# A graph attention layer on one Trainium2 core: the last score tile moves to ScalarE and GpSimd, mean and variance move to ScalarE, and half of the normalisation moves into the next step

## The chip, the cores and the metric

The kernel runs on one core of one Trainium2 chip. The metric is the device time of one execution in microseconds (us), the median over runs. The engines are named as in the profile: PE is TensorE, with PEld its weight loads, DVE is VectorE, ACT is ScalarE, POOL is GpSimd and SP is SyncE, which here only issues DMAs.

## The reference

For 16 graphs of N = 512 nodes with D = 384 features, 12 heads of E = 32, the layer computes (biases and constants left out where they play no part):

```python
h    = einsum('bnd,ade->bane', x, W)                      # features per head
th   = tanh(h)
attn = th @ w_src + swap(th @ w_dst)                      # one score per pair of nodes
attn = where(attn >= 0, attn, 0.2 * attn)                 # leaky
attn = softmax(where(adj, attn, -999))
out  = elu(einsum('banm,bame->bane', attn, h) + b)
gate = sigmoid(x @ H_w.T + H_b)
y    = x + gate * out + (1 - gate) * x
return (y - mean(y)) / sqrt(var(y) + 1e-5)                # over the 384 features
```

## The kernel before

One step handles one graph `b`, in C = 4 chunks of 128 nodes. There are 16 steps: `program` writes steps 0, 1, 14 and 15 out and loops over the others in pairs. Five engines each run their own fixed list of instructions; semaphores alone tie them together. Everything is software pipelined: in step `b` PE computes features of graph `b + 1` and gates of graph `b`, and what follows attention for graph `b - 1` (elu, gate mix, row sums, squares) is done in step `b`, with its normalisation in step `b + 1`.

**Score tiles.** For graph `b` the softmax numerators are 48 tiles of 128x512 (12 heads by 4 chunks), worked in 6 pairs of heads `j` (`edges`, L803). Tile t is one DVE instruction, `max(v, u) * adjacency` (L820), with the row `v` of a head spread over all partitions in `v_all` and the adjacency converted into PSUM by ACT. The tiles go through 16 slots (`ew`). PE multiplies each with the values (`attend`, L1068, L1082), ACT copies each pair's result (`copy_out`), PE transposes it, DVE divides (`attended`). Other DVE work is put between tiles by hand: `between` maps a place i of pair j to functions.

**From features to scores.** PE computes chunk 0 of the next graph's features at the head of a step, ACT takes the tanh (L471), POOL multiplies and halves (`weigh`, L296 and L302, four chunks), DVE reduces (`head_sums`, L782, at places between tiles), then the maximum over nodes (`scores_max`, L786). PE turns it (`max_T`, L1014) ahead of pair 2 of the attention.

**POOL's list in a step** (L386): four times `weigh`, the issue of a DMA that adds the bias, `subtract_x` and `mix` for graph `b - 1` (L339, L344, L347; the last of them writes `y` and waits for the store of the `y` before it), `add_rows` (L319, L323), `values`, `mean`, four times `split_low`, the issue of a second adding DMA, `variance`, `scale`. `add_rows` makes `hb_tot`, which PE reads in `means` (L1043, L1047). In PE's list `means` stands between the gates of chunk 3 and pairs 4 and 5 of the attention.

**SP's list** (L227): when `y` of graph `b - 1` is written, it loads `x_in`, stores the turned score rows to `v_rows`, waits until they have landed, and loads `v_all` for pairs 0, 1 and 2 of the next step (L220).

**ACT's list** (L580) holds tanh and copies of the features, two halves of `normalise` for graph `b - 2` around them, tanh and scaling of the gate, `copy_out`, copies of gates, `row_sums` and `row_squares` of graph `b - 1`, `split` and `adjacency`. The last step (`step_last` on each engine) has an order of its own and finishes graph 15 on DVE and POOL together.

Of the kernel before, what the change touches and what calls it, by code (L numbers as in the profile page):

```python
# [14 lines left out]
P = 128  # L15
# [6 lines left out]
def gat_layernorm(nc, x, xT, adjT, W, HwT, w_rows, bias, H_b, out):  # L22
# [23 lines left out]
    VB = 32  # L46
    assert N == 512 and H * E == D and B % 2 == 0

    ctx = ExitStack()
    with ctx:  # L50
# [6 lines left out]
        def sem(name):  # L57
# [7 lines left out]
        adj_in = sb("adj_in", [P, C, N], U8)  # L65

# [34 lines left out]
        u = sb("u", [P, 2, C, H])  # L101
        vals = sb("vals", [P, 2, C, H, VW])
# [49 lines left out]
            ew_ready ew_free outT_copied tr_done inv_done att_done  # L152
# [40 lines left out]
        def _(sp):  # L193
# [33 lines left out]
            def step(b, q, first, last, ahead=True):  # L227
# [11 lines left out]
                for j in range(VSLOTS, HP):  # L239
                    sp.wait_ge(S["ew_ready"], 4 * H * b + 2 * C * (j - 2))  # L240
                    load_v(b, q, j)
# [7 lines left out]
                if not last:  # L249
                    store_v(b + 1, 1 - q)  # L250
                    sp.wait_ge(S["st_v"], 64 * b + 128)
                    for j in range(VSLOTS):
                        if j:
                            sp.wait_ge(S["ew_ready"], 4 * H * b + 2 * C * (j + 4))
# [12 lines left out]
        def _(pool):  # L267
# [67 lines left out]

            def subtract_x(b):
# [24 lines left out]

# [4 lines left out]
            def step_last(b, q):  # L366
                subtract_x(b - 1)
# [15 lines left out]
                variance(b - 1)  # L383
                scale(b - 1)

            def step(b, q, first, last, ahead=True):  # L386
# [6 lines left out]
                if not last:  # L393
                    add_bias(b + 1)
                if first:
# [5 lines left out]
                if not last:  # L401
                    add_rows(b + 1, 1 - q)
                    values(b + 1, 1 - q)
                if not first:
                    mean(b - 1)
# [8 lines left out]
                if not first:  # L414
                    variance(b - 1)
                    scale(b - 1)
# [795 lines left out]
```

## Time and profile before

| what | value |
|---|---|
| median of 3 runs | 658.49 us (658.39 to 658.75) |
| the profiled execution, its own time | 658.69 us |
| its span, first to last instruction | 656.9 us |
| mean granted TensorE clock | 0.993 of 2.4 GHz |
| ACT busy | 429.6 us, 65% |
| chain that ended last | PE 48%, DVE 30%, issue 8%, POOL 7%, DMA 2%, ACT 2% |

The span is 1.79 us shorter than the profiled execution's own time. Busy time is the union of an engine's instructions; a matmul's end is modelled. Times of single instructions are counted from the start of the span, and L12 is line 12 of the kernel. "Rows" numbers in square brackets name the groups further down.

### The profile page before, as it was taken

The page shows a single profiled execution, that of the slowest core. Times are in us where ns is not written, and L with a number is a line of the kernel's source. Part 1 is how long each engine was busy: PE and PEld are TensorE (multiplying, and loading weights), DVE is VectorE, ACT ScalarE, POOL GpSimd, SP SyncE. Part 2 cuts the span into 40 slices and gives each one's busy share as a digit, 9 for nine tenths or more (in the row PEclk, how much of TensorE's full clock was granted, in tenths as well). Part 3 has the DMA queues.
Part 4 walks back from the last instruction along what each step waited for, and adds up shares of the span by engine and source line. Part 5 has one row for each costly group of instructions (what it writes and reads, how often), then busy time and mean ns, then how long its engine had stood idle before and what let it go on. Part 6 is the DMA issues. An engine that isn't in the chain of part 4 may idle for free.

```text
span 656.9 us, 12491 instructions
## 1 busy us (share of the span) xinstructions
PE 630.9 (96%) x3279; PEld 373.0 (57%) x3279; DVE 639.0 (97%) x1174; ACT 429.6 (65%) x936; POOL 571.4 (87%) x448
## 2 busy tenths in 40 slices
PE   8999999999999999999999999999999999999983
PEld 5565656574565647556664665656456565745531
DVE  7999999999999999999999999999999999999996
ACT  5434658486784848768485775848578584866664
POOL 2576998989989998998989999898999989997293
PEclk9999999999999999999999999999999999999997
DMA  6356549578475856848586584857747585675602
GB/s 209 118 131 181 178 123 274 128 196 248 140 235 129 235 164 176 240 146 251 133 210 190 154 238 144 249 132 200 228 142 233 139 259 126 187 211 131 217 40 97
DMA packets 54747, 117.62 MB, mean 179 GB/s; under 512 B 7106, under 2 KB 32452, under 8 KB 54724
## 3 DMA queue, kind: packets, MB, share of 16 engines
q1 hardware_dynamic: 42196, 81.56, 38.5%
q0 software_dynamic: 4320, 23.59, 19.2%
q10 hardware_dynamic: 8208, 12.19, 4.9%
q8 instruction: 11, 0.18, 0.1%
q14 instruction: 12, 0.10, 0.0%
HBM read 104.35 MB, written 12.98 MB: 179 GB/s over the span
## 4 chain that ended last, share of the span: by engine, by line
PE 48%; DVE 30%; issue 8%; POOL 7%; DMA 2%; ACT 2%; DVEq 1%; SPq 0%; POOLq 0%; ACTq 0%
PE out_T L1082 30%; DVE ew L820 20%; PE hg L982 13%; POOL th_w L296 4%; DVE sd L782 4%; DVE ex L842 3%; PE tr L1090 2%; POOL th_w L302 2%; PE hg L1047 1%; ACT th L471 1%; DMA xT_in<-in_xT 1%; DVE att L834 1%; DVEq L819 1%; PE hg L1014 1%; PE hg L1018 1%
## 5 line engine op out<-in xcount | busy, mean ns | idle before, releaser
L820 DVE SCALAR_TENSOR_TENSOR ew<-v_all,u,adj 128x512 f32<-128x512 f32 x768 | 522.7, 727 | 1.9 <-DMA v_all<-v_rows 1.2
L1082 PE MATMUL out_T<-ew,vals 128*64 128x512 f32 x1536 | 346.9, 597 | 0.0
L1082 PEld LDWEIGHTS out_T<-ew,vals 128*64 128x64 f32 x1536 | 106.3, 136 | 188.8 <-issue 144.1
L525 ACT ACTIVATE att_T<-out_T,out_bias 128x512 f32<-128x512 f32 x96 | 65.9, 686 | 116.1 <-PE out_T L1082 115.6
L296 POOL TENSOR_TENSOR th_w<-th,score_w 128x768 f32<-128x768 f32 x60 | 110.6, 1844 | 24.3 <-ACT th L471 24.3
L982 PE MATMUL hg<-w_hi,xT_hi 128*128 128x384 f32 x384 | 96.9, 360 | 0.8 <-ACT xT_hi L463 0.8
L982 PE MATMUL hg<-w_lo,xT_hi 128*128 128x384 f32 x384 | 88.2, 337 | 0.0
L982 PE MATMUL hg<-w_hi,xT_lo 128*128 128x384 f32 x384 | 87.7, 336 | 0.0
L302 POOL TENSOR_TENSOR th_w<-th_w 128x384 f32<-128x384 f32 x60 | 82.6, 1376 | 4.7
L982 PEld LDWEIGHTS hg<-w_hi,xT_hi 128*128 128x128 f32 x384 | 62.6, 189 | 40.2 <-issue 39.4
L982 PEld LDWEIGHTS hg<-w_lo,xT_hi 128*128 128x128 f32 x384 | 69.1, 188 | 0.0
L982 PEld LDWEIGHTS hg<-w_hi,xT_lo 128*128 128x128 f32 x384 | 68.9, 188 | 0.0
L333 POOL TENSOR_TENSOR vals<-h_sb,vals 128x384 f32<-128x384 f32 x64 | 53.3, 866 | 16.2 <-ACT vals L499 16.2
L339 POOL TENSOR_TENSOR ex<-ex,x_plus 128x1536 f32<-128x1536 f32 x15 | 56.4, 3758 | 11.4 <-ACT x_plus L530 11.4
L307 POOL TENSOR_TENSOR xT_lo<-xT_in,xT_hi 128x384 fp32r<-128x384 f32 x60 | 58.6, 1014 | 0.5 <-ACT xT_hi L463 0.5
L1090 PE MATMUL tr<-ident,att_T 128*128 128x128 f32 x384 | 53.1, 273 | 4.8 <-ACT att_T L525 4.8
L347 POOL TENSOR_TENSOR y<-x_in,ex 128x1536 f32<-128x1536 f32 x15 | 52.1, 3470 | 2.2 <-POOL ex L344 2.0
L344 POOL TENSOR_TENSOR ex<-gate,ex 128x1536 f32<-128x1536 f32 x15 | 52.0, 3467 | 1.4
L480 ACT ACTIVATE gate_tanh<-hg 128x384 f32<-128x384 f32 x60 | 29.5, 492 | 34.1 <-PE hg L982 32.8
L1090 PEld LDWEIGHTS tr<-ident,att_T 128*128 128x128 f32 x384 | 45.6, 141 | 10.8 <-ACT att_T L525 8.7
L471 ACT ACTIVATE th<-hg 128x384 f32<-128x384 f32 x64 | 31.7, 495 | 29.6 <-PE hg L982 29.6
L782 DVE TENSOR_REDUCE sd<-th_w 128x24 f32<-128x384 f32 (+1 forms) x64 | 36.5, 570 | 3.9 <-POOL th_w L302 3.7
(116 smaller groups left out, 669.0 us busy)
## 6 DMA issues: line engine op xcount, KB each, us to landing
v_all<-v_rows SPq DMA_DIRECT2D x95, 512.0 KB, 4.6
xT_in<-in_xT SPq DMA_DIRECT2D x16, 768.0 KB, 9.5
h_sb<-in_bias POOLq DMA_DIRECT2D x15, 768.0 KB, 6.7
x_in<-in_x SPq DMA_DIRECT2D x15, 768.0 KB, 4.6
gate_tanh<-in_H_b POOLq DMA_DIRECT2D x15, 768.0 KB, 9.4
out<-y ACTq DMA_DIRECT2D x15, 768.0 KB, 3.7
adj_in<-in_adjT SPq DMA_DIRECT2D x16, 256.0 KB, 9.8
v_rows<-v_turn SPq DMA_DIRECT2D x64, 6.0 KB
```

What stands on the lines that cost most here:

```text
L296: g.tensor_tensor(th_w[:, c % 2], th[:, c].unsqueeze(1).broadcast_to([P, 2, D]), score_w[:], ALU.mult).then_inc(S["thw_done"], 1)
L302: g.tensor_tensor(t[:, :, 0:E // 2], t[:, :, 0:E // 2], t[:, :, E // 2:E], ALU.add).then_inc(S["thh_done"], 1)
L307: g.tensor_tensor(xT_lo[:, q, :, n], xT_in[:, :, n], xT_hi[:, q, :, n].bitcast(F32), ALU.subtract).then_inc(S["xlo_done"], 1)
L333: g.tensor_tensor(o[:, :, 0:E], h_sb[:, c].rearrange("p (h e) -> p h e", e=E), o[:, :, E:E + 1].broadcast_to([P, H, E]), ALU.mult).then_in ...
L339: g.tensor_tensor(ex[:], ex[:], x_plus1[:], ALU.subtract).then_inc(S["mixed"], 1)
L347: g.tensor_tensor(y[:], x_in[:], ex[:], ALU.add).then_inc(S["mixed"], 1)
L525: a.activation(att_T[:, j % 2], OUT[j % 2][:], ACT.Identity, bias=out_bias[:, q, j:j + 1]).then_inc(S["outT_copied"], 1)
L782: ve.tensor_reduce(sd_ckh[:, 2 * H * c:2 * H * (c + 1)], t, AX.X, ALU.add).then_inc(S["sd_done"], 1)
L820: ve.scalar_tensor_tensor(out=twos(ew[:, (2 * C * j + i) % SLOTS, :]), in0=twos(v_all[:, j % VSLOTS, k]), scalar=u[:, q, c, h:h + 1], in1= ...
L982: last = te.matmul(o, l, r, start=(i == 0), stop=(i == len(mms) - 1))
L1082: te.matmul(OUT[j % 2][VW * k:VW * k + VW, :], vals[:, q, c, h, :], ew[:, t % SLOTS, :], start=(c == 0), stop=(c == C - 1)).then_inc(S["ew ...
L1090: last = te.transpose(TR[j % 2][:, c * P:(c + 1) * P], att_T[:, j % 2, c * P:(c + 1) * P], ident[:])
```

## The change

* **Tiles.** DVE makes 47 of the 48 tiles of a step (`EW` = 47). The last one (head 11, chunk 3) is made by ACT as Relu(v - u), then + u, after `copy_out` of pair 3, and POOL multiplies it with a bf16 copy of the adjacency, between `add_rows` and `values`. ACT makes that copy (`adjacency_side`) once a step. PE waits for POOL before that tile.
* **Mean and variance** become two ACT instructions (at the end of `row_sums` and of `row_squares`); POOL's three small ones go.
* **Next step.** Two of the four squares of `b - 1` move from the end of the step to where the second half of `normalise` stood in the next step. `scale` (power and shift) moves from the end of POOL's list to the next step, between the bias DMA and `subtract_x`; it runs in steps from 2 on. The whole `normalise` and the store of `y` move behind the copy of gate chunk 0.
* **Places on DVE.** In ordinary steps `head_sums` 0 goes one place later, `head_sums` 3 and `scores_max` one place earlier.
* **SP** counts 47 tiles, and the load for pair 2 also waits for ACT's part of the side tile.

```diff
+    SIDE = 1
+    EW = 4 * H - SIDE
...
+            def side_tiles(b):
+                pool.wait_ge(S["adj_side_done"], b + 1)
+                pool.wait_ge(S["side_scored"], 2 * SIDE * b + 2 * SIDE)
+                tiles = ew[:, SLOTS - SIDE:SLOTS, :]
+                g.tensor_tensor(tiles, tiles, adj_side[:].unsqueeze(1).broadcast_to([P, SIDE, N]), ALU.mult).then_inc(S["side_ready"], 1)
+
-            def mean(b):
-                pool.wait_ge(S["sums_done"], C * b + C)
-                g.tensor_tensor(neg_mean[:], sums[:], minus_share[:], ALU.mult).then_inc(S["mean_done"], 1)
-
-            def variance(b):
-                pool.wait_ge(S["squares_done"], C * b + C)
-                g.tensor_tensor(var[:], squares[:], share[:], ALU.mult).then_inc(S["var_done"], 1)
-                pool.wait_ge(S["var_done"], 2 * b + 1)
-                g.tensor_tensor(var[:], var[:], eps[:], ALU.add).then_inc(S["var_done"], 1)
-                pool.wait_ge(S["var_done"], 2 * b + 2)
-
             def scale(b):
-
+                pool.wait_ge(S["var_done"], b + 1)
+                if not isinstance(b, int) or b:
+                    pool.wait_ge(S["y_done"], C * b)
                 g.tensor_tensor(rstd[:], var[:], half[:], ALU.pow).then_inc(S["rstd_done"], 1)
                 pool.wait_ge(S["rstd_done"], 2 * b + 1)
                 g.tensor_tensor(shift[:], neg_mean[:], rstd[:], ALU.mult).then_inc(S["rstd_done"], 1)
 
             def step_last(b, q):
+                scale(b - 2)
...
+                if not isinstance(b, int) or b > 1:
+                    scale(b - 2)
...
                     add_rows(b + 1, 1 - q)
+                    side_tiles(b)
                     values(b + 1, 1 - q)
-                if not first:
-                    mean(b - 1)
...
-                if not first:
-                    variance(b - 1)
-                    scale(b - 1)
...
+            def side_tiles(b, q):
+                act.wait_ge(S["side_ready"], b)
+                a.activation(minus_u[:], u[:, q, C - 1, H - SIDE:H], ACT.Copy, scale=-1.0).then_inc(S["side_u"], 1)
+                act.wait_ge(ld_v[2], 32 * b + 32)
+                act.wait_ge(S["ew_free"], 4 * H * b + 4 * H)
+                act.wait_ge(S["side_u"], b + 1)
+                for i in range(SIDE):
+                    k = 2 - SIDE + i
+                    a.activation(ew[:, SLOTS - SIDE + i, :], v_all[:, 2, k], ACT.Relu, bias=minus_u[:, i:i + 1]).then_inc(S["side_scored"], 1)
+                for i in range(SIDE):
+                    h = H - SIDE + i
+                    act.wait_ge(S["side_scored"], 2 * SIDE * b + i + 1)
+                    a.activation(ew[:, SLOTS - SIDE + i, :], ew[:, SLOTS - SIDE + i, :], ACT.Identity,
+                                 bias=u[:, q, C - 1, h:h + 1]).then_inc(S["side_scored"], 1)
+
...
+                a.activation(neg_mean[:], sums[:], ACT.Copy, scale=-1.0 / D).then_inc(S["mean_done"], 1)
...
+                a.activation(var[:], squares[:], ACT.Identity, scale=1.0 / D, bias=eps[:, 0:1]).then_inc(S["var_done"], 1)
...
                 features(b + 1, 0)
-                if not isinstance(b, int) or b > 1:
-                    normalise(b - 2, 0, 2)
                 features(b + 1, 1)
                 elu_exp(b - 1, 1 - q)
                 features(b + 1, 2)
                 features(b + 1, 3)
                 if not isinstance(b, int) or b > 1:
-                    normalise(b - 2, 2, C)
+                    row_squares(b - 2, 2, C)
                 x_forms(b - 1)
                 gate_tanh_pass(b - 1)
                 copy_out(b, q, 0)
                 copy_out(b, q, 1)
                 gate_quarter_pass(b - 1)
                 gates(b, 0)
+                if not isinstance(b, int) or b > 1:
+                    normalise(b - 2)
                 gates(b, 1)
                 copy_out(b, q, 2)
                 exps(b + 1, 1 - q)
                 copy_out(b, q, 3)
+                side_tiles(b, q)
                 gates(b, 2)
                 row_sums(b - 1)
                 gates(b, 3)
...
-                row_squares(b - 1, 0, 2)
                 for c in range(2):
                     adjacency(b + 1, c)
+                adjacency_side(b + 1)
                 copy_out(b, q, 4)
-                row_squares(b - 1, 2, C)
+                row_squares(b - 1, 0, 2)
...
-                        put(5 if first else 1, lambda: head_sums(b + 1, 0))
+                        put(5 if first else 2, lambda: head_sums(b + 1, 0))
                         put(8 if first else 6, lambda: head_sums(b + 1, 1))
                     if j == 2 and not last:
                         put(3, lambda: head_sums(b + 1, 2))
-                        put(7, lambda: head_sums(b + 1, 3))
-                        put(8, lambda: scores_max(b + 1))
+                        put(7 if first else 6, lambda: head_sums(b + 1, 3))
+                        put(8 if first else 7, lambda: scores_max(b + 1))
...
-                        pe.wait_ge(S["ew_ready"], 4 * H * b + t + 1)
+                        if t < EW:
+                            pe.wait_ge(S["ew_ready"], EW * b + t + 1)
+                        elif t == EW:
+                            pe.wait_ge(S["side_ready"], b + 1)
```

## Rows read from the trace of the kernel before

**Rows 1.** The page: each engine's busy us, share of the span, instructions.

```profile
PE 630.9 (96%) x3279; PEld 373.0 (57%) x3279; DVE 639.0 (97%) x1174; ACT 429.6 (65%) x936; POOL 571.4 (87%) x448
```

**Rows 2.** Timeline of ACT: start, us, instruction, count, idle before and its end.

```profile
104.48 0.49 ACT L471 ACTIVATE th<-hg 128x384 f32<-128x384 f32 x1 [1.15 <-PE hg L982]
...
298.63 0.49 ACT L471 ACTIVATE th<-hg 128x384 f32<-128x384 f32 x1 [0.98 <-PE hg L982]
...
322.19 0.24 ACT L497 ACTIVATE s_pos<-d_rel 128x48 f32<-128x48 f32 x1
...
323.91 0.69 ACT L525 ACTIVATE att_T<-out_T,out_bias 128x512 f32<-128x512 f32 x1 [1.16 <-PE out_T L1082]
...
337.47 0.49 ACT L471 ACTIVATE th<-hg 128x384 f32<-128x384 f32 x1 [1.07 <-PE hg L982]
...
376.29 0.49 ACT L471 ACTIVATE th<-hg 128x384 f32<-128x384 f32 x1 [0.98 <-PE hg L982]
...
570.32 0.49 ACT L471 ACTIVATE th<-hg 128x384 f32<-128x384 f32 x1 [0.98 <-PE hg L982]
```

**Rows 3.** Waits of PE: us in total, times, longest.

```profile
PE hg L1014 <- DVE d_max_c L786: 8.3, 15, 0.7
```

**Rows 4.** Timeline of PE and of its weight loads.

```profile
82.95 0.33 PE L1014 MATMUL hg<-ident,d_max_c 128*128 128x128 f32 x1 [0.56 <-DVE d_max_c L786]
...
315.94 0.33 PE L1014 MATMUL hg<-ident,d_max_c 128*128 128x128 f32 x1 [0.49 <-DVE d_max_c L786]
...
327.64 0.81 PEld L1047 LDWEIGHTS hg<-mean_w,hb_tot 128*128 128x128 f32 x6
...
366.55 0.59 PEld L1047 LDWEIGHTS hg<-mean_w,hb_tot 128*128 128x128 f32 x4
```

**Rows 5.** Timeline of POOL, end of one step and the next.

```profile
296.73 1.03 POOL L362 TENSOR_TENSOR rstd<-var,half 128x4 f32<-128x4 f32 x1
297.84 0.20 POOL L364 TENSOR_TENSOR shift<-neg_mean,rstd 128x4 f32<-128x4 f32 x1
299.28 1.86 POOL L296 TENSOR_TENSOR th_w<-th,score_w 128x768 f32<-128x768 f32 x1 [1.24 <-ACT th L471]
...
304.12 2.55 POOL L302 TENSOR_TENSOR th_w<-th_w 128x384 f32<-128x384 f32 x1
...
313.04 3.78 POOL L339 TENSOR_TENSOR ex<-ex,x_plus 128x1536 f32<-128x1536 f32 x1
...
320.54 3.48 POOL L347 TENSOR_TENSOR y<-x_in,ex 128x1536 f32<-128x1536 f32 x1 [0.17 <-POOL ex L344]
...
325.90 1.02 POOL L323 TENSOR_TENSOR hb_tot<-hb_sum 128x384 f32<-128x384 f32 x1
```

**Rows 6.** Timeline of DVE.

```profile
302.27 0.55 DVE L782 TENSOR_REDUCE sd<-th_w 128x24 f32<-128x384 f32 x1 [0.30 <-POOL th_w L302]
...
304.05 1.75 DVE L842 SCALAR_TENSOR_TENSOR ex<-ex,att 128x1536 f32<-128x1536 f32 x1
...
328.57 9.37 DVE L820 SCALAR_TENSOR_TENSOR ew<-v_all,u,adj 128x512 f32<-128x512 f32 x14
...
333.90 0.75 DVE L820 SCALAR_TENSOR_TENSOR ew<-v_all,u,adj 128x512 f32<-128x512 f32 x1
```

**Rows 7.** DMA: SP's issues, then KB each and us from issue to landing.

```profile
329.55 4.70 SPq L220 DMA_DIRECT2D v_all<-v_rows  x3
...
v_all<-v_rows SPq DMA_DIRECT2D x1, 512.0 KB, 4.2
...
out<-y ACTq DMA_DIRECT2D x15, 768.0 KB, 3.7
```

**Rows 8.** Timeline of POOL and DVE near the end of the last step.

```profile
637.51 1.82 POOL L377 TENSOR_TENSOR ex<-ex,gate_tanh 128x768 f32<-128x768 f32 x1 [0.78 <-ACT ex L682]
...
641.37 1.82 POOL L382 TENSOR_TENSOR ex<-ex,x_plus 128x768 f32<-128x768 f32 x1
...
643.91 0.69 DVE L896 SCALAR_TENSOR_TENSOR ex<-ex,att 128x512 f32<-128x512 f32 x1 [0.21 <-ACT ex L686]
```

More of the change, by code:

```diff
@@ L65, in gat_layernorm @@
         adj_in = sb("adj_in", [P, C, N], U8)
+        adj_side = sb("adj_side", [P, N], BF16)
         w_hi = sb("w_hi", [P, KD, 2 * D], F32R)
@@ L101, in gat_layernorm @@
         u = sb("u", [P, 2, C, H])
+        minus_u = sb("minus_u", [P, SIDE])
         vals = sb("vals", [P, 2, C, H, VW])
@@ L239, in step @@
                 for j in range(VSLOTS, HP):
[L240 removed]
+                    sp.wait_ge(S["ew_ready"], EW * b + 2 * C * (j - 2))
                     load_v(b, q, j)
@@ L253, in step @@
                         if j:
-                            sp.wait_ge(S["ew_ready"], 4 * H * b + 2 * C * (j + 4))
+                            sp.wait_ge(S["ew_ready"], EW * b + min(2 * C * (j + 4), EW))
+                        if j == VSLOTS - 1:
+                            sp.wait_ge(S["side_scored"], 2 * SIDE * b + 2 * SIDE)
                         load_v(b + 1, 1 - q, j)
@@ L402, in step @@
                     add_rows(b + 1, 1 - q)
+                    side_tiles(b)
                     values(b + 1, 1 - q)
-                if not first:
-                    mean(b - 1)
                 if ahead:
@@ L413, in step @@
                 add_gate_bias(b)
-                if not first:
-                    variance(b - 1)
-                    scale(b - 1)
             def after():
@@ L442, in before @@
                     adjacency(0, c)
+                adjacency_side(0)
                 act.wait_ge(S["dve_setup"], DVE_SETUP)
@@ L503, in adjacency, with adjacency_side @@
                 if not isinstance(b, int) or b:
-                    act.wait_ge(S["ew_ready"], 4 * H * b - 2 * C + 4 * (c // 2) + 4)
+                    act.wait_ge(S["ew_ready"], EW * b + (0 if c // 2 else SIDE - C))
                 a.activation(ADJ_WORDS[c // 2][:, c % 2], adj_in[:, c].bitcast(U16), ACT.Copy).then_inc(S["adj_done"], 1)
+            def adjacency_side(b):
+                if not isinstance(b, int) or b:
+                    act.wait_ge(S["side_ready"], b)
+                a.activation(adj_side[:], adj_in[:, C - 1], ACT.Copy).then_inc(S["adj_side_done"], 1)
             def out_biases(b, q):
@@ L560, in row_sums @@
                     a.activation(scratch[:, c % 2], y[:, c], ACT.Copy, accum_out=sums[:, c:c + 1]).then_inc(S["sums_done"], 1)
+                act.wait_ge(S["sums_done"], C * b + C)
+                if not isinstance(b, int) or b:
+                    act.wait_ge(S["rstd_done"], 2 * b)
+                a.activation(neg_mean[:], sums[:], ACT.Copy, scale=-1.0 / D).then_inc(S["mean_done"], 1)
             def row_squares(b, lo=0, hi=C):
@@ L568, in row_squares @@
                                  accum_out=squares[:, c:c + 1]).then_inc(S["squares_done"], 1)
+                if hi < C:
+                    return
+                act.wait_ge(S["squares_done"], C * b + C)
+                if not isinstance(b, int) or b:
+                    act.wait_ge(S["rstd_done"], 2 * b)
+                a.activation(var[:], squares[:], ACT.Identity, scale=1.0 / D, bias=eps[:, 0:1]).then_inc(S["var_done"], 1)
             def normalise(b, lo=0, hi=C):
@@ L635, in step_first @@
                 gates(b, 3)
+                side_tiles(b, q)
                 for c in range(C):
@@ L641, in step_first @@
                 out_biases(b + 1, 1 - q)
+                adjacency_side(b + 1)
                 for c in range(2, C):
@@ L646, in step_last @@
             def step_last(b, q):
+                row_squares(b - 2, 2, C)
                 elu_exp(b - 1, 1 - q)
@@ L661, in step_last @@
                 copy_out(b, q, 3)
+                side_tiles(b, q)
                 exp_early(q)
@@ L809, in edges @@
                         break
+                    if 2 * C * j + i >= EW:
+                        continue
                     c, k = i // 2, i % 2
```

2 lines of the change are left out of this document (1 added, 1 removed).

## The prediction

> **What bounds the kernel now.** I read the page's busy shares first. DVE (97%) and PE (96%) are both nearly full, POOL is at 87% [rows 1]: no engine can be relieved alone, so the question is which chain of waits sets the step. The timeline of ACT gives the step: the tanh of feature chunk 0 starts at 104.48, 298.63, 337.47 and 570.32 [rows 2]. From 104.48 to 570.32 are 12 steps of 38.82 us; 298.63 to 337.47 is one of 38.84. I call this tanh's start F and count within a step from it.
>
> The waits of PE have one row that recurs every step: PE waits for the maximum from DVE 15 times, 8.3 us in all, 0.55 a time [rows 3]; its timeline shows 0.49 us of it before 315.94 [rows 4]. All else in PE's step is work, so PE alone would run a step in 38.82 - 0.55 = 38.27 us. DVE waits 0.30 us a step at the first reduction, which POOL's halving releases [rows 6]. The three engines turn in one ring: F, POOL's multiply and halving, DVE's reduction at F + 3.64 (302.27), the maximum and PE's turn at F + 17.31 (315.94), PE's list to the next F.
>
> What the rows also show is a second release of PE, which costs nothing yet. PE's `means` needs `hb_tot`. POOL ends it at 325.90 + 1.02 = 326.92, F + 28.29 [rows 5]; PE's weight loads for it start at 327.64, F + 29.01 [rows 4]. The margin is 0.72 us. From that load to the next F are 337.47 - 327.64 = 9.83 us of PE work without a gap (9.74 in the next step: 366.55 to 376.29) [rows 2, 4]. And POOL's list from F to `hb_tot` is without a gap: it waits 1.24 us for F, and later only 0.17 us between two dependent instructions [rows 5].
>
> **The change part by part.**
>
> *The side tile on DVE.* One instruction fewer. Fourteen in a row take 9.37 us [rows 6], so 0.67 us a step. It helps only if DVE's part of the ring sets the step.
>
> *The places on DVE.* Between the first reduction and the maximum lie 13 tiles in place of 15 (one leaves at the front, one at the back): 2 x 0.67 = 1.34 us less. Maximum ready at F + 17.31 - 1.34 = F + 15.97, while PE comes to it at F + 17.31 - 0.49 = F + 16.82. The wait of 0.55 us goes, and what is late next has to be looked for; it can be worth at most the 8.3 us of [rows 3].
>
> *`scale` ahead of `subtract_x`.* Power and shift, from 296.73 to 297.84 + 0.20 = 298.04, are 1.31 us of POOL [rows 5]. Before, they stood in the time in which POOL waits for F anyway (1.24 us of it was left over). Now they stand between F and `hb_tot`. `mean` and `variance`, which go, stood behind `hb_tot`, so their going doesn't pay it back. Lower bound for the move: nothing, if POOL had a hole there; the rows show none. Upper bound: 1.31 plus a wait for ACT's squares, which in ACT's list stand some 5 us earlier. I take 1.31. `hb_tot` is then ready at F + 28.29 + 1.31 = F + 29.60, and with 0.04 us for the semaphore PE loads at F + 29.64 and not at F + 29.01. The step is 29.64 + 9.83 = 39.47, in the other kind 29.64 + 9.74 = 39.38, mean 39.42: **0.60 us longer than 38.82**, although the wait for the maximum is gone. It needs no help from the step before: POOL, PE and F close this ring within one step.
>
> *ACT's three instructions for the side tile and POOL's multiply.* A 128x512 copy on ACT takes 0.69 us [rows 2]; two such and one of one column (a 48-column one took 0.24 [rows 2]) are 1.6 us, from about F + 26 to F + 27.6. Behind them in ACT's list stands the copy of gate chunk 2, for which `means` also waits; it would end near F + 28.1, before F + 29.6, so they are hidden by `hb_tot`. If that cover went they would be worth nothing still, since PE came at F + 29.01. POOL's multiply of 128x512 lies between a 128x384 one of 1.02 and a 128x768 one of 1.82 or 1.86 us [rows 5, 8]; I take 1.3. It stands behind `hb_tot`, and with 0.9 saved there on `mean` and `variance` and 1.24 of idle time POOL's own list comes to about 38.2 us a step, under 39.4. PE meets its result only at the 48th tile, some 5 us later.
>
> *Squares and normalisation.* On ACT the second half of the squares takes the place of the second half of `normalise`, equal in size. `normalise` and the store come behind gate chunk 0: rstd is ready near F + 15.7, four quarters end at F + 18.4, the store lands 3.7 us later [rows 7], at F + 22.1. The next `y` is written from F + 21.91 + 1.31 = F + 23.2 [rows 5]. The new wait stays 1.1 us short of mattering; but a bias DMA and a load of `v_all` fly at that time. I take 0, with 1 as the upper bound.
>
> *SP.* `y` ends 1.31 later, so do the stores and the load for pair 0: `y` end 324.02, issue 329.55, landing 4.2 later at 333.75, DVE's first tile at 333.90 [rows 5 to 7]. In the new step it lands at F + 36.43, some 3.0 before the next F; DVE reaches the reduction 7.6 later, at F + 4.6, and the maximum 12.3 after that, at F + 16.9. This is within 0.1 us of PE's arrival at F + 16.82 and well before the 0.6 us that PE loses at `means`. So DVE's lead is eaten by this load, but it costs nothing on top.
>
> *The ends.* Step 1 has no `scale`, so it gains the wait at 82.95: -0.56 [rows 4]. Then 12 steps at +0.60: +7.2. From the last F to the last step the load of pair 0 comes 1.3 us later, of which DVE's earlier place absorbs little: +1.0. In the last step ACT's side tile pushes the early elu 1.6 us back; POOL's three instructions started at 637.51 after a wait of 0.78 and the last was at 641.37 [rows 8]. Behind 1.3 us of POOL multiply and ACT's delay it starts near 642.9 and ends near 644.7, while DVE's elu at 643.91 [rows 8] needs the same port (below): +0.7. Sum: -0.56 + 7.2 + 1.0 + 0.7 = **+8.3 us**. The profiled execution took 658.69, which gives 667.0; the median of the runs is 0.20 lower, so 666.8.
>
> **The port.** One halving took 2.55 us, begun 0.07 after DVE's elu of 1.75 us; another instruction of its shape took 1.02 [rows 5, 6]. So 1.53 us of the F + 28.29 is POOL blocked by the elu. In the new step the elu would start near F + 5.6, and that halving at F + 5.49: now POOL is first. I assume that what the elu then waits it takes back from POOL's next instruction, so that POOL loses as much as before.
> The Trainium skill ("SBUF — State Buffer", section "Who interferes with whom") says that a VectorE instruction with two SBUF inputs and a GpSimd instruction that reads SBUF exclude each other, and that the one issued first holds the port to its end. The trace agrees for the order elu first. By that rule alone the halving would run in 1.02 and the elu would wait about 0.9 us on DVE, and whether POOL's next instruction or the elu gets the port decides; if POOL did, the time would be that of the first rival.
>
> **The rivals.**
>
> 1. *POOL gets the port back and PE becomes the bound: faster.* If the elu no longer blocks POOL, `hb_tot` comes at F + 28.1 and PE at F + 28.5, nothing holds PE and the 8.3 us of [rows 3] go: 658.7 - 8.3 + 0.7 = 651. For it: the elu comes later than the halving. Against: POOL's instructions follow each other without a hole until F + 14, so an elu of 1.75 us must push one of them. It decides from a saving on POOL of 0.63 us before `hb_tot`. Chance 0.12.
>
> 2. *The load of `v_all` alone: about the same or a little slower.* If `hb_tot` kept its margin by some overlap that I don't see, the ring over two steps would be left: `y` end F + 26.70, landing 9.73 later, 7.6 to the reduction, 12.33 to PE's turn, 21.53 to the F after: 77.9 for two steps, 38.95 each [rows 2 to 7]. 12 x 0.13 - 0.56 + 1.7 = +2.7, so 661. For it: every link is in the rows. Against: it spares `means`. Chance 0.10 for this and what else ends between 657.2 and 662.
>
> 3. *The store of `y` lands late: slower still.* If the store needs over 4.8 us beside the bias DMA and the load, all that exceeds it comes onto POOL before `hb_tot` and so onto each of 12 steps: 0.5 us make 6, so 673. For: 3.7 is a median of stores at another place. Against: 1.1 us of margin. Chance 0.13.
>
> 4. The early part could be off in my favour or against it without another mechanism (bounds of 0.04 for the semaphore and 1.25 to 1.35 for the move: +-0.8 us). That is within the forecast.
>
> **How the numbers follow.** Forecast (667, own range 664.5 to 669.5): 0.65. Rivals 1, 2 and 3: 0.12, 0.10, 0.13. About 0.2% (1.3 us) is what a measurement of this kernel can tell from no change. Faster by more: rival 1, 0.12, and a hundredth of rival 2: 0.13. Within: the lower part of rival 2, 0.05. Slower: 0.65 + 0.13 + the rest of rival 2 = 0.82. The range runs from 660.5, to hold rival 2's own time, to 673 for half of rival 3.
>
> **What would show it.** The distance from one tanh of chunk 0 to the next is 39.3 to 39.5; PE has a wait on `hb_tot` (POOL) of about 0.6 us a step and none on the maximum, or one under 0.1. Power and shift stand 14.4 to 15.7 us after the tanh. DVE waits for `v_all` about 1 us a step at pair 0. The store lands before POOL's `y` starts. It is wrong if PE's wait at `means` is absent and the step is 38.3 (rival 1), if the step is 38.9 with the wait still at the maximum (rival 2), or if POOL waits for the store before `y` (rival 3).

## The result and the profile after

| what | before | after |
|---|---|---|
| median of 4 runs | 658.48 us (658.39 to 658.75) | 690.00 us (683.86 to 696.92) |
| after / before | | 1.0447, 95% interval 1.0380 to 1.0514 |
| the profiled execution, its span | 658.69, 656.9 us | 683.86, 682.0 us |
| its mean granted clock | 0.993 | 0.987 |

The change makes the kernel 31.5 us slower; the forecast was 8.3. The profile fell on the fastest of the four runs; the others had a mean clock of 0.980, 0.975 and 0.972, and 690.38, 689.62 and 696.92 us. The ratio leaves out the slowest run, which lies over 1.5% above the fastest and counts as a slow one; the median has all four.

The page of the changed kernel, engines and three kinds of DMA (KB each, median us to landing):

```profile
PE 642.8 (94%) x3279; PEld 375.6 (55%) x3279; DVE 631.2 (93%) x1158; ACT 469.4 (69%) x1030; POOL 580.0 (85%) x419
...
POOL 42%; PE 29%; issue 16%; DVE 7%; ACT 3%; DMA 2%; POOLq 1%; SPq 0%; ACTq 0%; DVEq 0%
...
v_all<-v_rows SPq DMA_DIRECT2D x95, 512.0 KB, 4.5
...
h_sb<-in_bias POOLq DMA_DIRECT2D x15, 768.0 KB, 6.5
...
out<-y ACTq DMA_DIRECT2D x15, 768.0 KB, 4.9
```

No engine is as full as DVE and PE were [rows 1]: something makes all of them wait. The chain that ended last is now POOL for 42% (7% before). The store of `y` lands 4.9 us after its issue in the median, not 3.7 [rows 7]. The waits, of PE, POOL and DVE (us in total, times, longest):

```profile
PE hg L1086 <- POOL hb_tot L329: 17.8, 13, 3.1
...
PE hg L1053 <- DVE d_max_c L823: 1.6, 5, 0.4
```

```profile
POOL y L359 <- DMA out<-y: 14.9, 13, 3.8
```

```profile
DVE ew L859 <- DMA v_all<-v_rows: 28.4, 12, 4.6
```

PE waited 15 times for the maximum [rows 3]; now it waits at `means` for `hb_tot`. The new name is POOL's wait before `y` for the store of the `y` before it, in each of 13 steps. DVE's long row is a consequence: a late `y` means late loads for the next step.

**A usual step.** F is again the start of the tanh of chunk 0. Between the two tanhs stand the issues of the load of `v_all` for pair 5 and of the store of `y`:

```profile
309.25 0.49 ACT L473 ACTIVATE th<-hg 128x384 f32<-128x384 f32 x1 [0.96 <-PE hg L1021]
...
326.61 0.32 SPq L224 DMA_DIRECT2D v_all<-v_rows  x1
...
328.01 0.38 ACTq L610 DMA_DIRECT2D out<-y  x1
...
349.36 0.50 ACT L473 ACTIVATE th<-hg 128x384 f32<-128x384 f32 x1 [1.05 <-PE hg L1021]
```

POOL's list from the adding bias DMA to `hb_tot` in the same step, then PE's `means`:

```profile
323.09 0.87 POOL L317 DMA_DIRECT2D h_sb<-in_bias  x1
323.70 1.34 POOL L365 TENSOR_TENSOR rstd<-var,half 128x4 f32<-128x4 f32 x1
325.11 0.20 POOL L367 TENSOR_TENSOR shift<-neg_mean,rstd 128x4 f32<-128x4 f32 x1
325.27 3.47 POOL L351 TENSOR_TENSOR ex<-ex,x_plus 128x1536 f32<-128x1536 f32 x1
328.82 3.45 POOL L356 TENSOR_TENSOR ex<-gate,ex 128x1536 f32<-128x1536 f32 x1
333.10 3.50 POOL L359 TENSOR_TENSOR y<-x_in,ex 128x1536 f32<-128x1536 f32 x1 [0.83 <-DMA out<-y]
...
338.49 1.00 POOL L329 TENSOR_TENSOR hb_tot<-hb_sum 128x384 f32<-128x384 f32 x1
```

```profile
339.62 0.82 PE L1086 MATMUL hg<-mean_w,hb_tot 128*128 128x1 f32 x6 [1.19 <-POOL hb_tot L329]
```

The step is 349.36 - 309.25 = 40.11 us. `mix` starts at F + 19.57, where the forecast's move of 1.31 puts it (F + 18.26 before). The store is issued at F + 18.76, and `y` starts at F + 23.85, the first moment that it may: the store has taken 5.0 us. `hb_tot` ends at F + 30.24, `means` starts at F + 30.37, and the next F comes 9.74 later, as in [rows 2, 4]. So nearly all by which this step is longer than 39.42 (0.69 us) comes in at the store: POOL waits 0.83 there, where it had waited 0.17 before. (The power takes 1.34 us here and 1.03 in [rows 5], `subtract_x` 3.47 and 3.78: the two differences cancel, and the move is worth the 1.31 all the same.)

**Two unusual steps.** In the steps that begin at 143.94 and 588.84 POOL waits 3.52 and 3.79 us before `y`. The two issues, POOL and PE in the first of them:

```profile
162.19 0.32 SPq L224 DMA_DIRECT2D v_all<-v_rows  x1
162.62 0.39 ACTq L610 DMA_DIRECT2D out<-y  x1
```

```profile
170.43 3.52 POOL L359 TENSOR_TENSOR y<-x_in,ex 128x1536 f32<-128x1536 f32 x1 [3.52 <-DMA out<-y]
```

```profile
176.94 0.82 PE L1086 MATMUL hg<-mean_w,hb_tot 128*128 128x1 f32 x6 [2.95 <-POOL hb_tot L329]
177.70 8.78 PE L1124 MATMUL out_T<-ew,vals 128*64 128x512 f32 x32
```

The three transfers that are open then, first in the usual step, then in this one (each the answer for one stretch):

```profile
h_sb<-in_bias POOLq DMA_DIRECT2D x1, 768.0 KB, 6.8
out<-y ACTq DMA_DIRECT2D x1, 768.0 KB, 5.0
v_all<-v_rows SPq DMA_DIRECT2D x1, 512.0 KB, 4.5
```

```profile
h_sb<-in_bias POOLq DMA_DIRECT2D x1, 768.0 KB, 6.5
out<-y ACTq DMA_DIRECT2D x1, 768.0 KB, 7.7
v_all<-v_rows SPq DMA_DIRECT2D x1, 512.0 KB, 6.6
```

The usual step issues the load for pair 5 at 326.61, 1.40 us ahead of the store (328.01); this one at 162.19, 0.43 us ahead of it (162.62). The step at 588.84 has 0.28 us and a landing after 8.1. The traces of four kernels in which both transfers are whole (this one and experiments 2, 3 and 7) have 52 such stores. The 12 that went out 1.4 us behind the load landed in 4.7 to 5.1 us; of the 19 at 0.6 to 0.8 us behind it, 16 took 6.2 to 6.7 and three 7.3 to 8.6; the 21 at 0.1 to 0.4 us took 6.7 to 8.1. So as a rule the store takes longer the nearer it is behind the load, and the two unusual steps are those in which the load went out late. What made it late there was not looked into.

**The clock.** Granted clock after that wait (columns: stretch, us, busy us of PE, PEld, DVE, ACT, POOL with counts, clock, DMA share, GB/s):

```profile
177.00:179.00 2.00, 2.00 (x12) 1.17 (x14) 2.00 (x4) 1.93 (x9) 2.00 (x3) 1.00 0.64 216
179.00:182.40 3.40, 3.40 (x10) 0.97 (x8) 0.53 (x1) 1.20 (x4) 3.40 (x5) 0.50 0.60 158
```

For 3.41 us PE runs at 1.2 GHz in place of 2.4, and the 32 matmuls of pairs 4 and 5 take 8.78 us where the usual step has 7.09: 1.69 us lost. This happens three times (179.01, 219.97, 622.74); before, the clock was full from 100 to 648 us. (Both kernels have one more stretch at half the clock, of some 10 us, right at their end.)

The sum against the forecast: the first F comes at 65.24, 0.35 earlier than before; the 13 distances to 588.84 are 18.9 longer; the rest, 682.0 - 588.84 = 93.16 against 656.9 - 570.32 = 86.58, is 6.6 longer. Together +25.1.

### The profile page after: what moved, and what is told of

Read it like the earlier page. It is cut to its first block, busy times and chain, and to the rows that moved or that the text cites. A ratio compares the mean times of both kernels' runs of the same rounds, so it can differ in the third digit from the quotient of the medians.

```text
span 682.0 us, 12625 instructions
## 1 busy us (share of the span) xinstructions
PE 642.8 (94%) x3279; PEld 375.6 (55%) x3279; DVE 631.2 (93%) x1158; ACT 469.4 (69%) x1030; POOL 580.0 (85%) x419
## 4 chain that ended last, share of the span: by engine, by line
POOL 42%; PE 29%; issue 16%; DVE 7%; ACT 3%; DMA 2%; POOLq 1%; SPq 0%; ACTq 0%; DVEq 0%
PE out_T L1124 19%; POOL th_w L302 15%; PE hg L1021 7%; POOL ex L356 6%; POOL ex L351 6%; POOL th_w L308 4%; POOL hb_sum L325 4%; DVE ew L859 3%; POOL rstd L365 2%; POOL hb_tot L329 2%; POOL h_sb L317 2%; PE hg L1086 2%; DMA out<-y 1%; ACT th L473 1%; DVE sd L819 1%
## 5 line engine op out<-in xcount | busy, mean ns | idle before, releaser
L859 DVE SCALAR_TENSOR_TENSOR ew<-v_all,u,adj 128x512 f32<-128x512 f32 x752 | 513.8, 728 | 34.1 <-DMA v_all<-v_rows 28.4
L1124 PE MATMUL out_T<-ew,vals 128*64 128x512 f32 x1536 | 357.2, 604 | 0.0
L1124 PEld LDWEIGHTS out_T<-ew,vals 128*64 128x64 f32 x1536 | 110.1, 138 | 195.4 <-issue 139.7
L302 POOL TENSOR_TENSOR th_w<-th,score_w 128x768 f32<-128x768 f32 x60 | 113.7, 1896 | 25.9 <-ACT th L473 25.9
L308 POOL TENSOR_TENSOR th_w<-th_w 128x384 f32<-128x384 f32 x60 | 79.3, 1322 | 4.7
L359 POOL TENSOR_TENSOR y<-x_in,ex 128x1536 f32<-128x1536 f32 x15 | 52.4, 3492 | 15.0 <-DMA out<-y 14.9
L351 POOL TENSOR_TENSOR ex<-ex,x_plus 128x1536 f32<-128x1536 f32 x15 | 52.5, 3497 | 8.1 <-ACT x_plus L552 8.1
L605 ACT ACTIVATE y<-y,shift,rstd 128x384 f32<-128x384 f32 x60 | 37.5, 696 | 8.2 <-POOL shift L367 8.2
```

Source lines behind the costliest of these rows:

```text
L302: g.tensor_tensor(th_w[:, c % 2], th[:, c].unsqueeze(1).broadcast_to([P, 2, D]), score_w[:], ALU.mult).then_inc(S["thw_done"], 1)
L308: g.tensor_tensor(t[:, :, 0:E // 2], t[:, :, 0:E // 2], t[:, :, E // 2:E], ALU.add).then_inc(S["thh_done"], 1)
L351: g.tensor_tensor(ex[:], ex[:], x_plus1[:], ALU.subtract).then_inc(S["mixed"], 1)
L359: g.tensor_tensor(y[:], x_in[:], ex[:], ALU.add).then_inc(S["mixed"], 1)
L859: ve.scalar_tensor_tensor(out=twos(ew[:, (2 * C * j + i) % SLOTS, :]), in0=twos(v_all[:, j % VSLOTS, k]), scalar=u[:, q, c, h:h + 1], in1= ...
L1124: te.matmul(OUT[j % 2][VW * k:VW * k + VW, :], vals[:, q, c, h, :], ew[:, t % SLOTS, :], start=(c == 0), stop=(c == C - 1)).then_inc(S["ew ...
```

## The experiments

Each ratio is against runs of the kernel before that were made together with those of the experiment; their median was 659.29 us for 1, 2, 3 and 8, 658.61 for 4, 7, 9 and 10, and 658.48 for 5, 6 and 11.

**1. Power and multiply alone.** To the kernel before, two POOL instructions of `scale`'s shapes at its new place; nothing else.

```diff
                 if not last:
                     add_bias(b + 1)
+                if not isinstance(b, int) or b > 1:
+                    g.tensor_tensor(spare[:, 0], eps[:], half[:], ALU.pow).then_inc(S["spare_done"], 1)
+                    pool.wait_ge(S["spare_done"], 2 * b - 3)
+                    g.tensor_tensor(spare[:, 1], spare[:, 0], half[:], ALU.mult).then_inc(S["spare_done"], 1)
```

> The kernel before, with a power and a dependent product of 128x4 (1.31 us) added to POOL between the bias DMA and subtract_x from step 2 on; their result is used nowhere. Theory (POOL's work ahead of hb_tot moves PE at its means): hb_tot ends near F + 29.6 and not F + 28.3, PE waits for it about 0.6 us a step, the step grows from 38.8 to about 39.4 and the time to 665 to 668, with up to 5 us more if the idle PE also loses its clock now and then. Rival (the 25 us and more come from the side tile and its waits): POOL's hole before F takes it, 658 to 660.

Measured: 667.77 us (667.05 to 669.56), ratio 1.0138 (1.0117 to 1.0158). PE's waits:

```profile
PE hg L1019 <- DVE d_max_c L791: 10.2, 15, 1.0
...
PE hg L1052 <- POOL hb_tot L324: 2.7, 10, 0.3
```

The clock is full. Ten of the twelve steps take 39.3 to 39.5 us, and in them `hb_tot` ends at F + 29.5 to 29.6 and `means` starts 0.13 to 0.14 us later: this step of the forecast has its mechanism and its size (29.60, 29.64). The wait at `means` is only 0.3 us and not 0.6, since the places on DVE are not moved here and PE still waits for the maximum first. The other two steps take 39.75 and 39.85 us: PE waits 1.0 us for the maximum in them and not at all for `hb_tot`.

**2. The late normalisation alone.** To the kernel before, all of `normalise` and the store behind gate chunk 0.

```diff
                 features(b + 1, 0)
-                if not isinstance(b, int) or b > 1:
-                    normalise(b - 2, 0, 2)
...
                 features(b + 1, 3)
-                if not isinstance(b, int) or b > 1:
-                    normalise(b - 2, 2, C)
...
                 gates(b, 0)
+                if not isinstance(b, int) or b > 1:
+                    normalise(b - 2)
```

> The kernel before, with all four quarters of normalise and the store of y behind the copy of gate chunk 0; nothing else. Theory: the store is issued near F + 18.0, behind the load of v_all for pair 5 (F + 17.1), and lands at F + 22.7 to 23.2, so POOL's write of y (F + 21.9) waits 0.8 to 1.3 us; hb_tot has 0.7 us of margin, so the step grows by 0.1 to 0.6 us: 660 to 668. Rival (the store is early enough, its wait is only seen because POOL was late): no wait on the store and 658 to 660.

Measured: 694.71 us (691.56 to 699.39), ratio 1.0562 (1.0518 to 1.0606), far above every expectation. POOL's and PE's waits:

```profile
POOL y L347 <- DMA out<-y: 37.7, 13, 4.8
```

```profile
PE hg L1045 <- POOL hb_tot L323: 21.8, 13, 3.6
```

The store's issues and their median to landing:

```profile
out<-y ACTq DMA_DIRECT2D x15, 768.0 KB, 6.4
```

In a usual step the load for pair 5 is issued at F + 17.2 and the store at F + 17.9, 0.7 us behind it, and the store lands 6.4 us later, at F + 24.3: although it goes out 0.9 us earlier than in the changed kernel it lands 0.5 us later. `y`, without `scale` ahead of it, is there sooner and waits 2.9 us a time in the mean. Steps from 2 on are 40.4 to 42.3 us, and the clock halves four times for 3.41 us. This edit alone costs more than the whole change.

**3. Both edits of 1 and 2.**

> The kernel before with both: the 1.31 us on POOL and the late normalise and store. Theory: here the late store is hidden behind POOL's own lateness, since y starts at F + 23.2 and the store lands near there (its start does not hang on POOL's power): the prices do not add, 666 to 672. If they add (0.6 and 1.1 a step) the time is 675 to 685, and the changed kernel's 684 to 697 is explained without the side tile.

Measured: 701.0 us (698.89 to 701.68), ratio 1.0624 (1.0601 to 1.0646). POOL's and PE's waits:

```profile
POOL y L348 <- DMA out<-y: 28.4, 13, 3.3
```

```profile
PE hg L1050 <- POOL hb_tot L324: 23.9, 13, 3.1
```

POOL's wait is shorter by 9.3 us than in 2, PE's is longer by 2.1. In the usual steps the two instructions start `mix` 1.23 us later, and all of this is hidden in the wait for the store: `y` starts at F + 24.3, `hb_tot` ends at F + 30.7, and with the clock full the step takes 40.4 to 40.6 us, in 2 and in 3. What 3 loses beyond 2 is lost in other steps. In six of its twelve steps the load goes out only 0.24 us ahead of the store (in one of 2), and the store then takes 6.9 to 7.9 us; and the clock halves six times, not four. In total the prices of 1 and 2, 8.5 and 35.4 us, give 43.9, against 41.7 measured: the intervals don't tell this from plain addition, though the steps show that it is none. Both expectations missed, for the reason found in 2.

**4. A quarter of the store.** The changed kernel; the store writes the first quarter of `y` alone, the rest of the output is left out.

```diff
-                act.dma_start(out_v[b], y[:]).then_inc(S["st_y"], 16)
+                act.dma_start(out_v[b][:, 0], y[:, 0]).then_inc(S["st_y"], 16)
```

> The changed kernel, but the store of y in steps 2 to 15 writes its first quarter only (three quarters of the output are left out). Theory (late store, then POOL's y, then hb_tot, then PE at means): the store lands well before F + 23.2, POOL's wait for it (0.5 to 3.8 us a step) is gone, what is left is the 1.31 us of POOL; the time is that of the kernel before with that work alone, 666 to 670, and the runs scatter by 2 us and not by 13. Rival (the store's wait is a small part and the rest is ACT's or the side tile's): 677 or more.

Measured: 669.63 us (666.28 to 671.25), ratio 1.0150 (1.0122 to 1.0179). Of POOL's wait for the store 4.8 us over 4 times remain; PE's and DVE's waits:

```profile
PE hg L1086 <- POOL hb_tot L329: 8.0, 13, 1.5
```

```profile
DVE ew L859 <- DMA v_all<-v_rows: 19.8, 12, 2.6
```

Nine of the twelve steps have no wait for the store. They take 39.2 to 39.3 us, with 0.49 to 0.54 at `means`, where the forecast had 39.42 and 0.63. In the other three and in the last part the quarter store takes 5.4 to 5.5 us and POOL waits 1.2 to 1.3; in those three steps it is again 0.4 us behind the load. With the same instructions on every engine, three quarters of the store were worth 20 of the 31 us. The 11 that are left hold the price of `scale`, these four waits and, in the profiled run, one halving of the clock.

**5. and 6. Which neighbour delays the store?** Both start from experiment 2. In one the load for pair 5 brings one partition (heads 10 and 11 come from other rows), in the other the adding bias DMA one partition (the bias is left out elsewhere).

```diff
-                    load_v(b, q, j)
+                    if j == HP - 1:
+                        sp.dma_start(v_all[0:1, j % VSLOTS], v_rows[q, 2 * j:2 * j + 2, :].rearrange("(o k) n -> o k n", o=1)).then_inc(ld_v[j % VSLOTS], 16)
+                    else:
+                        load_v(b, q, j)
```

> The kernel of b_store_late, but the load of v_all for pair 5 brings one partition (4 KB and not 512; heads 10 and 11 are computed from other rows). Theory A (the store of y, issued 0.7 us behind that load, shares the DMA engines with it): it lands 3.7 to 4.9 us after its issue and not 6.4, POOL's wait for it falls from 2.6 to under 1 us a step: 660 to 672. Theory B (it is the adding bias DMA, issued at F + 13.7 and landing at F + 20.4): no change, 6.4 us and 690.

```diff
-                pool.dma_start(h_sb[:].rearrange("p c d -> p (c d)"), bias_rows, accum_op=ALU.add).then_inc(S["add_bias_done"], 16)
+                pool.dma_start(h_sb[0:1].rearrange("p c d -> p (c d)"), bias_rows[0:1], accum_op=ALU.add).then_inc(S["add_bias_done"], 16)
```

> The kernel of b_store_late, but the adding bias DMA brings one partition (6 KB and not 768; the bias is left out elsewhere). Theory A (the load for pair 5 holds the store up): the store still lands over 5.5 us after its issue, POOL waits over 2 us a step, 685 or more. Theory B (the bias DMA): it lands within 4.5 us and the time is 660 to 672. If both transfers count, each of the two runs takes back a part.

Measured, one run each: 663.43 and 679.05 us, against 694.71. POOL's wait and the store's landing with the small load:

```profile
POOL y L350 <- DMA out<-y: 12.7, 13, 2.5
```

```profile
out<-y ACTq DMA_DIRECT2D x15, 768.0 KB, 4.6
```

The same with the small bias DMA:

```profile
POOL y L347 <- DMA out<-y: 31.2, 13, 3.2
```

```profile
out<-y ACTq DMA_DIRECT2D x15, 768.0 KB, 5.6
```

Both transfers count, the load about twice as much: the landing falls from 6.4 us by 1.8 with it and by 0.8 with the bias DMA, together nearly the 2.7 that it lies above the 3.7 of [rows 7]. In time 31 us of 36 go with the load and 16 with the bias DMA. That is more than 36 together because PE's margin of 0.7 us at `means` swallows the first part of any wait: with the small load most steps are back at 38.8 to 38.9 us although POOL still waits 0.4 to 1.0. The small load also takes work off SP's queue, and DVE's wait for `v_all` falls from 33.3 to 5.1 us, so a part of its 31 may not be the store's. One run each has no interval; the waits and landings carry the order.

**7. `means` later.** The changed kernel with `means` between pairs 4 and 5, which gives `hb_tot` about 3.5 us.

```diff
-                means(b + 1, 1 - q)
-
                 attend(b, q, 4)
+                means(b + 1, 1 - q)
                 attend(b, q, 5)
```

> The changed kernel with PE's means behind pair 4 of the attention instead of ahead of it. Theory: PE no longer stands still for hb_tot and keeps its clock; what is left is the chain over two steps from y's end over the load of v_all to DVE's maximum, 26.7 + 0.6 + 9.6 + 0.1 + 7.5 + 12.3 + 21.5 = 78.3 us for two steps, so 39.2 a step: 662 to 672, with no granted clock at half inside the steps. Rival (POOL's lateness reaches PE by other ways just as strongly, or the store's wait grows by as much): 680 or more.

Measured: 711.99 us (709.27 to 713.56), ratio 1.0807 (1.0776 to 1.0837). POOL's and DVE's waits:

```profile
POOL y L359 <- DMA out<-y: 39.8, 14, 3.7
POOL th_w L302 <- DVE sd L819: 20.6, 12, 1.7
```

```profile
DVE ew L859 <- DMA v_all<-v_rows: 38.1, 11, 4.6
```

PE no longer waits at `means`. The first step with a store is 38.8 us, as without the change, but the others are 42 to 43. I read this from the waits: `y` still ends only when the store lets it; the loads for the next step come after `y`, DVE's first tiles after the loads, its reductions at F + 6.7 and F + 12.9, and POOL's fourth multiply waits 1.7 us for the second of them, so that `scale`, the next store and the next `y` are late too. The store is now 0.2 us behind the load for pair 5 and takes 6.7 to 7.9 us. So the store closes a ring of its own over DVE, which PE's wait had kept slack. No experiment takes this ring apart. My expectation missed; the rival in it held.

**8. The side tile alone.** The changed kernel with `scale` at the end of POOL's list, all squares in their own step, `normalise` and the store where they were. Tile, statistics on ACT and places on DVE stay.

```diff
-                if not isinstance(b, int) or b > 1:
-                    scale(b - 2)
...
                 add_gate_bias(b)
+                if not first:
+                    scale(b - 1)
...
-                if not isinstance(b, int) or b > 1:
-                    row_squares(b - 2, 2, C)
+                    normalise(b - 2, 2, C)
...
-                row_squares(b - 1, 0, 2)
+                row_squares(b - 1)
```

> The changed kernel with power and shift at the end of POOL's list, all squares in their own step and normalise with its store at its places in the kernel before. Left of the change: the side tile, mean and variance on ACT, the places on DVE. Theory: hb_tot is back at F + 28.3, nothing new stands ahead of it, the wait for the maximum is gone (0.55 us, 15 times) and PE is the bound: the step is 38.3 and the time 650 to 652. Rival (the side tile costs by itself): 658 or more, with a wait for side_ready or for the copies of gates behind ACT's side work.

Measured: 659.26 us (657.56 to 660.43), ratio 0.9997 (0.9986 to 1.0008). Steps are 38.63: the wait for the maximum is gone, but only 0.19 of 0.55 us is kept. DVE's and POOL's waits:

```profile
DVE ew L857 <- ACT adj L521: 5.5, 11, 0.6
```

```profile
POOL rstd L365 <- ACT var L599: 9.5, 14, 4.2
```

The side tile, the second adjacency copy and the statistics make ACT's list late, so the adjacency in PSUM comes 0.5 us too late for DVE's fifth tile of pair 0. The rest went in the last part (89.2 against 86.6 us); 1.7 of these 2.6 us are one halving of the clock in the profiled run (615.92).

**9. and 10. ACT's order.** Experiment 8 with the adjacency ahead of the squares; and that with all 48 tiles of the last step on DVE.

```diff
                 copy_out(b, q, 4)
-                row_squares(b - 1)
                 for c in range(2, C):
                     adjacency(b + 1, c)
+                row_squares(b - 1)
```

> The kernel of a_side_only (the change without its part on scale, squares and store) with ACT converting adjacency 2 and 3 ahead of the squares. Theory: there DVE waited 0.5 us a step for that conversion, came late to the tiles of pair 3 and starved PE by 0.4 us; with it gone the step falls from 38.6 to 38.3: 652 to 656. Rival (it is the load of v_all that holds DVE): the wait moves to the load, 658 to 660.

> As a_side_adj, and in the last step DVE makes all 48 tiles (no side tile there). Theory: the last step of a_side_only was 2.6 us longer than before, since ACT's side work pushes the early elu back; this gives 1 to 2.6 us: 650 to 655. Rival (the last step's length has another cause, a lower clock): no difference from a_side_adj.

Measured: 660.87 (660.63 to 662.33), ratio 1.0039 (1.0026 to 1.0051), and 659.91 (659.77 to 660.47), ratio 1.0020 (1.0011 to 1.0030). Both missed, though 10 is 1.0 us faster than 9, at the lower end of the 1 to 2.6 that it was to bring. POOL's wait in the second:

```profile
POOL rstd L365 <- ACT var L598: 18.6, 14, 4.9
```

DVE's wait for the adjacency is gone and POOL's for the variance has doubled; its `weigh` then starts late, and steps are 38.8 to 39.1. This order doesn't help: the stretch of ACT's list is full. In experiment 8 ACT is busy for 12.57 of the 13.00 us from F + 25 to F + 38, where it was for 10.86 before.

**11. Work out of the full stretch.** Experiment 8 with the bf16 adjacency copied early, in ACT's idle time near F + 17, into two buffers; a bf16 scratch for the sums; the last step all on DVE.

```diff
-        adj_side = sb("adj_side", [P, N], BF16)
+        adj_side = sb("adj_side", [P, 2, N], BF16)
-        scratch = sb("scratch", [P, 2, D])
+        scratch = sb("scratch", [P, 2, D], BF16)
...
-            def adjacency_side(b):
-                if not isinstance(b, int) or b:
-                    act.wait_ge(S["side_ready"], b)
+            def adjacency_side(b, q):
+                act.wait_ge(S["ld_adj"], 16 * b + 16)
+                if not isinstance(b, int) or b > 1:
+                    act.wait_ge(S["side_ready"], b - 1)
```

> The kernel of a_side_only with the bf16 copy of the adjacency made in ACT's idle time near F + 17 (two buffers for it; the scratch tile of the row sums in bf16 to make room) and all 48 tiles of the last step on DVE. Theory (ACT's list between F + 25 and F + 38 was full: in a_side_only DVE waited 0.5 us a step for the adjacency, in a_side_adj POOL waited 1.3 us for the variance): both waits go, PE is fed, the step is 38.3 to 38.5 and the time 650 to 655. Rival (the load of v_all for pair 0, behind y and the stores, holds DVE): the waits move to that load and the time stays at 657 to 660.

Measured: 653.98 us (652.86 to 655.05), ratio 0.9927 (0.9913 to 0.9940): faster than both kernels. PE's and DVE's waits:

```profile
PE hg L1050 <- DVE d_max_c L820: 1.1, 3, 0.4
```

```profile
DVE ew L856 <- PE out_T L1121: 4.5, 9, 1.2
```

From the second step with a store on, steps are 38.3 to 38.4, near the 38.27 that the prediction reads for PE alone. The gain has two parts: the last step on DVE alone is worth about 1 us by experiments 9 and 10, the rest goes with the early copy. The bf16 scratch tile only makes room; ACT's sums and squares take 0.51 and 0.60 us with either type.

## Why the prediction was wrong

**Right: what bounds the kernel and what the places do.** The wait for the maximum goes (8.3 us to 1.6), and PE then has to wait at `means`, as forecast.

**Right: the price of `scale`.** Forecast: hb_tot 1.31 later, 0.60 a step. The changed kernel has `mix` at F + 19.57, where 18.26 and the move of 1.31 put it; experiment 1 has 39.3 to 39.5 us in ten of twelve steps and 667.8 us in all; the nine steps of experiment 4 without a wait for the store have 39.2 to 39.3, a little under the forecast. The 0.04 us for the semaphore stands in no row; the runs show 0.13 to 0.14 us from the end of `hb_tot` to `means`.

**Wrong: the store.** The failed step is "the store lands 3.7 us later, at F + 22.1 ... I take 0, with 1 as the upper bound". The issue time was right within 0.4 us (F + 18.76 against 18.4). The landing was not: 4.7 to 5.1 us in the usual steps, 7.7 and 8.1 in two. The 3.7 was a median of stores that were issued at another point of the step. The sentence even names the bias DMA and the load that fly there, and then prices them at nothing. Experiments 2, 5 and 6 show that they are the cause. Rival 3 had the mechanism, and the sign that the prediction names for it, a wait of POOL before `y`, is the one that came. Its 0.5 us a step was right for the usual step too: outside the two unusual ones POOL waits 0.69 us a time, 0.52 more than the 0.17 of before. What rival 3 lacked, and why its 673 is too low, are the two steps with over 3.5 us each, and the clock.

The excess of the profiled run over the forecast is 25.1 - 8.3 = 16.8 us. POOL's 14.9 us before `y`, less 13 times the 0.17 that it waited there anyway [rows 5], is 12.7; three clock losses of 1.7 are 5.1; together 17.8, so the account is 1.0 us too large, and where that is lost stays open. Of the 12.7, 5.7 fall on eleven usual waits and 7.0 on the two long ones. The store's wait passes to F nearly one to one because the chain from `y` over `hb_tot` and `means` has no slack left, and that is the forecast's own finding.

**Not foreseen: the clock.** No step of the prediction prices what PE's idle time does to its clock. In the changed kernel it halves three times, 0.8 to 2.1 us behind the start of a `means` that had waited 2.95, 1.15 and 3.14 us. It halves four and six times in experiments 2 and 3, each time 0.5 to 2.1 us behind a `means` that had waited 1.1 to 3.6 us. It halves once each in 4 to 8, always behind the last F, and never before the closing stretch of the kernel before or of experiments 1, 9, 10 and 11. Such a wait isn't enough by itself: usual steps with 1.2 us, and steps of experiments 2 and 3 with 2.2 to 2.4, don't show it. The median lies 6.1 us above the profiled run, and all three slower runs have a lower mean clock than it. One stretch of 3.41 us is 3.41 x 0.5 / 690 = 0.0025 of the mean clock, so the 0.007 to 0.015 that those runs have less stand for 3 to 6 more such stretches, an estimate of 5 to 10 us. What in a single run decides whether a wait is followed by such a stretch stays open; so does whether the longer waits in those runs come first.

**The port.** In the unusual step that begins at 143.94 and in the usual one that begins at 309.25, POOL, then DVE's elu:

```profile
149.46 1.01 POOL L308 TENSOR_TENSOR th_w<-th_w 128x384 f32<-128x384 f32 x1
150.43 3.35 POOL L302 TENSOR_TENSOR th_w<-th,score_w 128x768 f32<-128x768 f32 x1
...
314.73 2.64 POOL L308 TENSOR_TENSOR th_w<-th_w 128x384 f32<-128x384 f32 x1
```

```profile
149.93 2.16 DVE L881 SCALAR_TENSOR_TENSOR ex<-ex,att 128x1536 f32<-128x1536 f32 x1
...
314.75 1.75 DVE L881 SCALAR_TENSOR_TENSOR ex<-ex,att 128x1536 f32<-128x1536 f32 x1
```

At 314.7 both start within 0.02 us, and the halving is held up and takes 2.64 us in place of 1.02. At 149.5 the halving came first and took 1.01; the elu then needed 0.41 more than 1.75, and the multiply behind it 1.52 more than its 1.83. POOL loses 1.5 to 1.6 us either way, as assumed, so nothing of rival 1 came from this side. The Trainium skill ("SBUF — State Buffer", section "Who interferes with whom") says that whichever of the two engines issued first holds the port to its end. The row at 149.5, where the halving is 0.47 us ahead and the elu ends late, agrees, and so do [rows 5, 6] for the other order; at 314.7 the starts are too close to tell the order.

**The ends.** Forecast -0.56 for step 1, measured -0.35. For the last part forecast +1.7, measured +6.6: the step that begins at 588.84 is one of the two with a late store (3.8 us at `y`), and one clock loss (622.74) lies there. Rival 2's load ring shows as DVE's wait (28.4 us); as far as the waits tell, it sets the step in experiment 7 alone, and there together with the store.

**The wrong expectations of the experiments.** Number 8 was to give the side tile's gain of 8 us; it asked what comes ahead of `hb_tot` and not whether ACT, at 65% of the whole run, has room where the new work is due. From F + 25 to F + 38 ACT's list is full, and 9 and 10 only moved the wait from DVE to POOL. Number 11, which moves work out of that stretch and the side tile out of the last step, gets 4.5 us of the 8.3.

## What to carry to other kernels

A landing time read from a profile belongs to the point at which the transfer was issued. Before moving a transfer, list what else is in flight at the new point, read the landing of large transfers that already share such a stretch, and take that for the price if anything waits for it: here 4.7 to 8.1 us in place of 3.7, on a chain that the same change had just made critical. An engine with 65% busy time can be full in the one stretch where the new work is due, and here the way to the gain was to move work to another stretch; putting it into another order within the full one brought nothing.

## What the runs showed of the hardware

In the kernel before a 768 KB store from SBUF landed 3.4 to 4.3 us after issue, 3.7 in the median. Issued 1.4 us behind a 512 KB load and about 5 us behind a 768 KB adding DMA it took 5.0, and 0.4 us behind the load 7.7; the load itself then took 6.6 in place of 4.5. Thirteen times, in the changed kernel and experiments 2 and 3, the granted clock fell to 1.2 GHz for 3.41 us, 0.5 to 2.1 us behind the start of a `means` that had waited 1.1 to 3.6 us; where it was taken apart, one such stretch cost 1.7 us. Waits of up to 2.4 us also passed without it. A ScalarE conversion of 128x512 into bf16 took 0.63 us, a GpSimd multiply of 128x512 1.16 where I took 1.3.
